# Masks of two eight-expert layers added by 128-row matmuls over zeros, from one copy of the mask

## The reference

```python
# L2_ffn (in the kernel: moe2)
logits = x @ Wr + br;  probs = softmax(logits)
idx = argmax(probs);   gate = max(probs)            # tokens over an expert's capacity get gate 0
h = relu(einsum('ecd,edf->ecf', expert_in, W1) + b1[:, None, :])
eo = einsum('ecf,efd->ecd', h, W2) + b2[:, None, :] # times gate, back to the token's place
# L3_ffn (in the kernel: moe3)
logits = xf @ Wg + bg; idx = argmax(softmax(logits))
h = gelu(einsum('th,ehi->tei', xf, W1) + b1)
y = einsum('tei,eih->teh', h, W2) + b2
out = take_along_axis(y, idx)                       # the chosen expert's row
```

## Time and profile before

| | us |
|---|---|
| median of 3 runs | 2430.18 |
| lowest and highest of them | 2424.86, 2434.6 |
| the profiled execution's own time | 2427.39 |
| its span, first to last instruction | 2425.6 |
| mean granted TensorE clock in it | 0.991 of full |
| TensorE busy (matmul) | 2312.0 |
| VectorE, ScalarE, GpSimd busy | 1490.3, 1163.5, 916.8 |

### The profile page before, as it was taken

How to read it: one execution, slowest core, us unless ns; L and a number is a source line. 1 busy time by engine, 2 the same in 40 slices (tenths; PEclk the granted TensorE clock), 3 DMA queues, 4 the chain that set the end, 5 groups by cost and what they waited for, 6 DMA issues and landing times.

```text
span 2425.6 us, 41921 instructions
## 1 busy us (share of the span) xinstructions
PE 2312.0 (95%) x16426; PEld 1567.8 (65%) x16426; DVE 1490.3 (61%) x4040; ACT 1163.5 (48%) x2998; POOL 916.8 (38%) x853
## 2 busy tenths in 40 slices
PE   9999989999989999999999999999999999999998
PEld 6766656666766665666666675666666666666665
DVE  6457566666575567666564567756665555665653
ACT  5544334555445533445644453545555445354543
POOL 5334353433234336434332444543323243544310
PEclk9999999999999999999999999999999999999999
DMA  5000000000000000000000000000000000000000
GB/s 235 1 1 1 1 14 1 10 1 27 1 1 1 1 1 10 18 10 1 19 1 1 1 1 5 10 14 10 10 5 1 1 1 1 1 1 1 2 1 14
DMA packets 6821, 26.57 MB, mean 11 GB/s; under 512 B 864, under 2 KB 992, under 8 KB 5984
## 3 DMA queue, kind: packets, MB, share of 16 engines
q1 hardware_dynamic: 6624, 23.89, 2.7%
HBM read 21.79 MB, written 2.10 MB: 10 GB/s over the span
## 4 chain that ended last, share of the span: by engine, by line
PE 75%; DVE 16%; issue 3%; ACT 3%; POOL 3%; DMA 0%; POOLq 0%; DVEq 0%; SPq 0%
PE ps L486 9%; PE ps L499 8%; PE ps L549 7%; PE ps L518 6%; PE ps L510 4%; PE ps L889 4%; PE ps L628 4%; PE ps L603 3%; PE ps L471 3%; PE ps L596 3%; PE ps L650 3%; PE ps L601 3%; PE ps L677 2%; PE ps L846 2%; DVE P L1405 2%
## 5 line engine op out<-in xcount | busy, mean ns | idle before, releaser
L1919 POOL TENSOR_TENSOR P<-P,small 128x384 f32<-128x384 f32 x384 | 316.1, 845 | 564.0 <-DVE small L1430 564.0
L1140 ACT ACTIVATE P<-ps,small 128x192 f32<-128x192 f32 x768 | 315.0, 425 | 134.3 <-DVE small L1422 132.8
L1892 POOL TENSOR_TENSOR small<-small,mhalf 128x4 f32<-128x4 f32 x112 | 126.5, 1130 | 511.9 <-DVE small L1410 255.2
L499 PE MATMUL ps<-kvT,big 128*128 128x192 f32 x1536 | 311.4, 333 | 4.5 <-DVE big L1439 1.8
L499 PEld LDWEIGHTS ps<-kvT,big 128*128 128x128 f32 x1536 | 248.8, 190 | 74.9 <-issue 45.1
L1422 DVE TENSOR_REDUCE small<-ps 128x2 f32<-128x384 f32 x384 | 208.3, 550 | 108.8 <-PE ps L499 100.4
L486 PEld LDWEIGHTS ps<-wts,P 128*128 128x128 f32 x1920 | 232.3, 192 | 45.3 <-issue 30.6
L486 PE MATMUL ps<-wts,P 128*128 128x128 f32 x1920 | 247.8, 278 | 3.8 <-DVE P L1827 2.1
L2009 POOL TENSOR_TENSOR P<-T 128x512 f32<-128x512 f32 x96 | 125.4, 1306 | 197.2 <-DVE T L1709 128.2
L518 PEld LDWEIGHTS ps<-value,big 128*128 128x128 f32 x1536 | 178.6, 192 | 28.3 <-issue 18.6
L518 PE MATMUL ps<-value,big 128*128 128x128 f32 x1536 | 188.0, 278 | 0.1
(11 more groups left out here) (287 smaller groups left out, 4495.6 us busy)
## 6 DMA issues: line engine op xcount, KB each, us to landing
ctok<-ctok_dram SPq DMA_DIRECT2D x8, 512.0 KB, 4.1
ctxT<-ctx_dram SPq DMA_DIRECT2D x8, 512.0 KB, 4.1
wts<-weights_dram SPq DMA_DIRECT2D x1, 2530.0 KB, 23.3
wts<-weights_dram SPq DMA_DIRECT2D x1, 2189.0 KB, 17.8
X<-x_dram SPq DMA_DIRECT2D x8, 256.0 KB, 3.5
big<-fold_dram SPq DMA_DIRECT2D x2, 1024.0 KB, 8.5
out_dram<-X SPq DMA_DIRECT2D x8, 256.0 KB, 2.3
wts<-weights_dram SPq DMA_DIRECT2D x1, 1536.0 KB, 25.8
```

The lines of the kernel that those rows point to most:

```text
L499: m = pe.matmul(ps[s][:, at:at + KEYS], big[s][:, BANK * b + 128 * p:BANK * b + 128 * p + 128], kvT[s][:, keys_at(b):keys_at(b) + KEYS], s ...
L1140: m = act.activation(probs(s, b // 2)[:, to:to + KEYS], ps[s][:, at:at + KEYS], ACT.Exp, bias=small[s][:, 4 * e + p:4 * e + p + 1], accum_ ...
L1892: pool.tensor_tensor(rstd(s, name, n), variance(s, name, n), mhalf[:, 0:n], ALU.pow).then_inc(*sig("rstd", s))
L1919: m = pool.tensor_tensor(view, view, over(small[s][:, at:at + 2], 2, [128, 2, KEYS]), ALU.mult)
```

## The change

The second copy of the mask goes: ScalarE writes `mTb` at partitions 0 to 7 alone. Both buffers `mTb` are set to zero once in the setup, over all 128 partitions, and `pick_b` is cast in one instruction over 128 partitions, whose rows from 8 on are zero for every expert. The mask matmul then takes all 128 rows of both. `fold_dve` is raised once less, and TensorE's wait goes from 5 to 4.

```diff
                 def moe1(s, i):
                     yield
                     if i == 0:
-                        pe.wait_ge(fold_dve, 5)
+                        pe.wait_ge(fold_dve, 4)
...
                 def mask(s, e, first):
-                    p0 = 32 * (e % 2)
-                    return pe.matmul(bank(s, U3[e % 3]), pick_b[p0:p0 + EXPERTS, 128 * e:128 * e + 128], mTb[s][p0:p0 + EXPERTS, :],
-                                     start=first, stop=not first)
+                    return pe.matmul(bank(s, U3[e % 3]), tile_of(pick_b, e), mTb[s][:, :], start=first, stop=not first)
...
                     rows_ = bank(s, k, 1, 0, EXPERTS)
-                    for p0 in (0, 32):
-                        act.activation(mTb[s][p0:p0 + EXPERTS, :], rows_, ACT.Copy, scale=-NEG, bias=NEG)
+                    act.activation(mTb[s][0:EXPERTS, :], rows_, ACT.Copy, scale=-NEG, bias=NEG)
                     act.activation(tmp(s, 3)[0:EXPERTS, :], rows_, ACT.Copy).then_inc(*sig("zT", s))
...
                     dve.tensor_copy(upto_b[:, :], C("upto"))
-                    for p0 in (0, 32):
-                        dve.tensor_copy(pick_b[p0:p0 + 32, :].rearrange("p (e m) -> p e m", m=128),
-                                        over(C("ident")[p0:p0 + 32, p0:p0 + EXPERTS], 2, [32, EXPERTS, 128])).then_inc(fold_dve, 1)
+                    for t in range(SLOTS):
+                        dve.memset(mTb[t][:, :], 0.0)
+                    dve.tensor_copy(pick_b[:, :].rearrange("p (e m) -> p e m", m=128),
+                                    over(C("ident")[:, 0:EXPERTS], 2, [128, EXPERTS, 128])).then_inc(fold_dve, 1)
```

## The result

The changed kernel takes 2432.95 us (median of 22 runs, 2425.24 to 2435.69) where the kernel before took 2424.92 beside it (22 runs, 2421.17 to 2434.68): a ratio of 1.0029 with an interval of [1.0019, 1.0038]. That is slower: the whole interval lies above 1, though single runs of one kernel scatter by 10 us and more, and the difference is less than 0.5%. I had forecast 2429.6, a gain of 0.6 us that nobody could measure.

The account below looks back on a forecast made before the run. TensorE, busy 95% of the span, was taken as the bound. Masks +0.7, ScalarE −1.2 and setup −0.1 summed to −0.6 us against the median of 2430.18, so 2429.6 was forecast, range 2421 to 2437.

Parts of the forecast that it names:

- Part 1, the masks: Mask matmuls on TensorE at 128 rows: gains and losses by following instruction sum to +0.7 us, bounds −5 and +15.
- 15 × 0.20: Fifteen mask pairs followed by L908, the bias over 8 rows: +0.20 us each, +3.0 in the sum.
- the two unhindered pairs ahead of L492: Among four mask pairs followed by L492 or L478, forecast to come out even.
- Part 2, ScalarE: Sixteen evacuations go from ScalarE: −1.2 us where TensorE waits for it, bounds 0 and −9.4.
- the 0.6 at 713: TensorE's wait at 713.79 for Z of L1115, queued behind L1213 and L1252: −0.59 us.
- The other two places: Waits for L1167 of L518 at 1732.46 and L510 at 1795.12: about −0.3 us each.
- Part 3, setup: VectorE's setup, one cast at 0.70 and two memsets at 0.3 against 1.39: net −0.1 us, ends −0.5 and +1.0.
- The clock, the rival at 0.06: Shifted stream may bring or save stretches at the lower clock: past 12 us, chance 0.04 faster, 0.02 slower.
- the 12 us: About 0.5% of the time, what a measurement of this kernel can tell from no change.
- 3.4 us for a stretch: Cost of the low-clock stretch at 932 to 939, 0.49 × 7; four such were to pass 12 us.
- the sum of −0.6: Whole kernel: +0.7 for masks, −1.2 for ScalarE, −0.1 for setup; forecast as no change, chance 0.81.

Follow-up runs that it names:

- `bias_128`: Changed kernel with the bias matmuls also over all 128 rows: 2426.22 us, ratio to the kernel before 0.9992 [0.9983, 1.0001].
- `two_copies`: Changed kernel with ScalarE writing both copies of the mask again: 2428.38 us, ratio to the kernel before 1.0005 [0.9996, 1.0014].
- `before_late`: Kernel before with two memsets of mTb added ahead of the casts in the setup: 2426.97 us, ratio 0.9989 [0.9977, 1.0001].
- the fourth session: Kernel before, nothing edited, timed beside the two kernels with filled waits: 2432.40 us (9 runs), mean clock 0.9891.
- `after_late`: Changed kernel with its setup memsets issued twice, each waiting for the last: 2428.92 us, ratio to the kernel before 1.0000 [0.9991, 1.0009].

## Why the prediction was wrong

**Part 1, the masks: the step before L908 was mis-sized.** Every step that I read from L645 and L467 holds: 0.43 before the masks, 0.22 in the pair, none behind it, 0.31 before L650 and L755. The term "15 × 0.20" of the sum is what failed. It took the new entry into L908 as one step of 0.10, read from L650, whose four matmuls start together behind a single step. L908 starts one at a time, and its second matmul pays another 0.10, just as the second L486 does on the way back, which I had in the sum. From the last `up` to the second L908 it was 0.53 + 0.22 + 0.11 = 0.86 and is 0.43 + 0.22 + 0.31 + 0.21 = 1.17: +0.31 in 15 places, 4.6 in place of 3.0. A smaller miss runs the other way: the two unhindered pairs ahead of L492, which I called even, gain 0.09 each, since they too lose a step on the way back (the second L492 starts 0.13 behind the first in the kernel before and 0.03 in the changed one, at 1911). TensorE's sum is then +2.1, not +0.7. `bias_128`, which removes the entry steps and the steps behind L906 with them, gains 4.2 to 4.6 us.

**Part 2, ScalarE: a place gave nothing.** Of the forecast −1.2, the 0.6 at 713 did not come, for a reason that I should have asked for: what is late next. It is L1252, which cannot run before L725 of TensorE itself is done, and the instruction that writes Z is queued behind it. The other two places came, in the timeline of PE: from L471 to L510 it was 0.87 at 1794.25 and is 0.44 at 1795.94, the wait gone; and L518 behind the pair of 1732 no longer waits. About −0.7 in all, and `two_copies` measures 0.3 to 0.8.

**Part 3, setup:** −0.4 where I had −0.1, within my ends of −0.5 and +1.0. The cast over 128 partitions takes 0.62, as a single one over 32 does (33.81 in the timeline of `before_late`), and the memsets 0.27 each, where I had 0.70 and 0.3.

The three corrected terms, +2.1 − 0.7 − 0.4 = +1.0, stand against 0.4 to 0.9 measured at one clock. So the sum of −0.6 was wrong in sign, by 1.6 us: the second entry step is 1.6 of it, and the other corrections (−0.2, +0.5 and −0.3) cancel.

**The clock, the rival at 0.06, stood in the sum as nothing.** It is the larger of the two steps that failed: of the 8 us, 2.7 go with a mean clock that is lower by 0.0014 over all runs whose clocks are known. It is far from the 12 us to which I had tied its chance. Its price was off too: I took 3.4 us for a stretch, from the one at 932, and four stretches for 12 us. Most stretches are half as long as that one (0.0007 of the mean clock each), and by the measured slope such a one costs 1.3, so that 12 us would take about nine. I named its mechanism ("the new form moves the stream by tenths of a microsecond, which may bring such a stretch or save one") and then forecast the median as if the program kept its mean clock. The runs show that it does not: 0.9888 for the changed kernel, in both of its sessions, 0.9904 for the kernel before beside it in the second, 0.9921 with two memsets more. Nor is the mean clock a property of the program alone, as 0.9891 in the fourth session shows. For an edit of 1 us, the uncertainty of the median should have been some ±4 us from this alone (an estimate from the clocks of 0.9888 to 0.9921 and the slope), with the mean of the forecast unchanged. The sign of this part could not be forecast from the profile.

What stays open: what in the change brings which stretch. `two_copies` and `after_late` have the same masks as the changed kernel and a clock of 0.991, so it is not the masks as such. And 4.5 of the first 8 us, more than half, were the low time of the kernel before in that session. Its clocks are not known; the slope would ask for a mean of about 0.992, which is an estimate and not shown.

## What to carry to other kernels

A price at a change of row group has as many steps as there are instructions that pay it: read the second instruction behind the edge as well as the first, on the way in as on the way out, and from an instruction that starts in the same manner. Where one kind of matmul is moved to 128 rows, move its small neighbours with it, since a neighbour left behind takes over the edges (here +0.31 each until L906 followed). Before a gain or loss of a few microseconds is believed, put the times beside the mean granted clock of each run; and where TensorE is the bound and stands for 1 to 3 us, try a few matmuls into a free bank in that wait: here they gained 10 us, where the best edit of the work gained 4.6.

## What the runs showed of the hardware

- The mean granted clock, given to three digits, explains the times to 0.7 us: 1.86 us per 0.001, over 233 runs from 2414 to 2439 us.
- The clock can fall behind waits of TensorE of 1.09 and 0.69 us (before L471 at 701.52 and L492 at 702.86, ahead of the stretch at 704) and can stay up behind one of 1.76 us (1695 in the kernel before).
- An 8-row f32 matmul behind 128-row ones costs 0.10 at its start and the second one 0.10 more (0.309 and then 0.214 from start to start, by the trace's own start times; 0.216 and 0.11 in `bias_128`, where the rows don't change).
- Two 8-row masks of one row group are 0.226 apart, in two row groups 0.004; two 128-row masks are 0.216 apart.
- VectorE casts 1024 columns to bf16 in 0.62 over 128 partitions and in 0.62 over 32.
